# A two-layer graph network on one core: overflow check, record format and the order in which a one-hot stage begins

## The reference

```python
# layer 0: per edge (row = src, col = dst), w = exp(-edge_weight)
h   = relu(layernorm(x))
x   = x + relu(h @ WS.T + bS + segment_sum((h[dst] @ WN.T + bN) * w[:, None], src))
# layer 1: attention over the edges that end in a node
h   = relu(layernorm(x))
q, k, v = h @ Wq + bq, h @ Wk + bk, h @ Wv + bv
logit = sum(q[dst] * k[src]) / sqrt(128)        # softmax over the edges of each dst
x   = x + elu(segment_sum(alpha[:, None] * v[src], dst) + h @ Ws + bs)
```

## Time and profile before

| | |
|---|---|
| median of 3 executions | 880.79 us (880.11 to 882.0) |
| profiled execution | 879.39 us |
| its span, first to last instruction | 877.6 us |
| TensorE busy | 770.2 us (88%) |
| VectorE busy | 725.2 us (83%) |
| ScalarE busy | 530.8 us (60%) |
| PoolE busy | 255.2 us (29%) |
| mean granted TensorE clock | 0.973 |

### The profile page before, as it was taken

How to read it: one execution, slowest core, us unless ns; L and a number is a source line. 1 busy time by engine, 2 the same in 40 slices (tenths; PEclk the granted TensorE clock), 3 DMA queues, 4 the chain that set the end, 5 groups by cost and what they waited for, 6 DMA issues and landing times.

```text
span 877.6 us, 23043 instructions
## 1 busy us (share of the span) xinstructions
PE 770.2 (88%) x8849; PEld 664.7 (76%) x8896; DVE 725.2 (83%) x883; ACT 530.8 (60%) x1034; POOL 255.2 (29%) x200
## 2 busy tenths in 40 slices
PE   0073899999999999999999777899999999999996
PEld 0052777777777777777776556799999999999996
DVE  6657999999999999999995635778878878878872
ACT  5954767676676766767665352455564565555554
POOL 5640000000000000000000320557657657656666
PEclk9996799999999999999999899899999999999999
DMA  9440113132131311313123602204334334324400
GB/s 231 140 131 2 77 78 150 75 131 94 75 149 75 140 84 84 140 75 149 75 93 132 262 38 75 76 2 156 112 122 155 112 121 155 127 106 155 144 18 11
DMA packets 17516, 94.96 MB, mean 108 GB/s; under 512 B 2594, under 2 KB 8844, under 8 KB 10956
## 3 DMA queue, kind: packets, MB, share of 16 engines
q1 hardware_dynamic: 14428, 89.18, 26.6%
q0 software_dynamic: 3056, 5.35, 2.5%
HBM read 50.31 MB, written 44.21 MB: 108 GB/s over the span
## 4 chain that ended last, share of the span: by engine, by line
PE 66%; DVE 16%; issue 10%; ACT 4%; POOL 1%; DMA 1%; DVEq 1%; POOLq 0%; SPq 0%; ACTq 0%
PE bank L1167 16%; PE bank L1177 14%; PE bank L1027 13%; DVE oh_key L872 6%; PE bank L1017 5%; PE bank L1089 5%; PE bank L1087 4%; PE bank L1164 3%; DVE kT L776 3%; PE bank L1131 2%; PE bank L1136 1%; ACT kT L510 1%; ACT qT L502 1%; DVE mx L948 1%; DVE oh_lo L869 1%
## 5 line engine op out<-in xcount | busy, mean ns | idle before, releaser
L456 POOL TENSOR_TENSOR sm<-sm,mbc 128x896 f32<-128x896 f32 (+1 forms) x100 | 186.0, 1892 | 47.2 <-ACT mbc L646 47.2
L1087 PE MATMUL bank<-oh_key,oh_lo 128*128 128x100 bf16 x1600 | 173.5, 210 | 12.7 <-DVE oh_key L872 11.4
L1027 PE MATMUL bank<-wsb,hvb 128*128 128x512 f32 (+1 forms) x350 | 165.2, 577 | 14.4 <-DVE kT L776 13.2
L1167 PE MATMUL bank<-qT,kT 128*128 (+1 forms) x1250 | 170.6, 278 | 3.6 <-DVEq L170 1.2
L1089 PE MATMUL bank<-oh_key,oh_lo 128*128 128x50 bf16 x3200 | 173.7, 188 | 0.0
L1167 PEld LDWEIGHTS bank<-qT,kT 128*128 128x128 f32 x1250 | 167.5, 195 | 5.0
L1087 PEld LDWEIGHTS bank<-oh_key,oh_lo 128*128 128x128 bf16 x1600 | 156.6, 98 | 18.7 <-DVE oh_key L872 11.6
L1089 PEld LDWEIGHTS bank<-oh_key,oh_lo 128*128 128x128 bf16 x3200 | 167.0, 98 | 1.1
L650 ACT ACTIVATE sm<-sm 128x896 f32<-128x896 f32 (+1 forms) x100 | 86.7, 867 | 108.9 <-POOL sm L456 108.9
L552 ACT COPY wsb<-bank 128x512 f32<-128x512 f32 (+1 forms) x175 | 87.9, 552 | 106.2 <-PE bank L1017 106.2
L1177 PE MATMUL bank<-vals,sm 128*128 128x129 f32 x1250 | 147.5, 274 | 0.2 <-ACT sm L650 0.2
(11 more groups left out here) (120 smaller groups left out, 725.4 us busy)
## 6 DMA issues: line engine op xcount, KB each, us to landing
gt<-gst SPq DMA_DIRECT2D x25, 1600.0 KB, 5.6
gl_sb<-gt SPq DMA_DIRECT2D x25, 1600.0 KB, 6.7
records<-rec SPq DMA_DIRECT2D x1, 1612.0 KB, 6.1
out<-res SPq DMA_DIRECT2D x24, 64.0 KB, 1.6
dst_i<-in_dst SPq DMA_DIRECT2D x1, 403.0 KB, 5.8
dstn_i<-in_dst_next SPq DMA_DIRECT2D x1, 403.0 KB, 6.8
src_i<-in_src SPq DMA_DIRECT2D x1, 403.0 KB, 7.3
w_in<-in_edge_weight SPq DMA_DIRECT2D x1, 403.0 KB, 8.0
```

Of the source, the lines that this page charges most:

```text
L456: pool.tensor_tensor(part, part, mbc[:, v % 2:v % 2 + 1, :].to_broadcast([P, n, P]), ALU.subtract).then_inc(sub_done, 1)
L1027: T.matmul(ps(6 + at)[:, 0:n], hvb[:, w, :], wsb[:, at, 0:n], start=True, stop=True).then_inc(l0_mm, 1)
L1087: T.matmul(cells, lo, oh_key[:, u, m, 0:2 * KEYS, i], start=True, stop=False, skip_group_check=True)
L1167: ins = T.matmul(score_bank(g)[:, j * P:(j + 1) * P], kT[:, (a + j) * P:(a + j + 1) * P], qT[:, bass.ds(t * P, P)], start=False, stop=True ...
```

## The change

- **The check.** The host gives a third array, `dst_far`: the destination of the edge 128 further on. VectorE marks edges for which it is not above their own destination with the lowest bit set, and edges whose successor is lower. ScalarE sums both marks, TensorE adds the sums, and the flag is written before any window is fetched. `open_windows` has no `over` any more, and a window is 128 records.
- **The branch.** Each engine reads the flag and branches where it stands; `end_stage(1)` is gone, and a new barrier, `start_slow`, is in the slow branch alone.
- **The records.** Five fp32 words (20 bytes in place of 16): key (destination times 25 plus the high source bits), low bits, three weight parts. The windows are transposed as fetched, by a view of the upper half of each word; VectorE only subtracts the pair's offset from the keys.
- **The layer norm.** ScalarE does the sums and squares of 17 tiles, VectorE the other eight with its batch-norm statistics.
- **The order.** One-hots begin when block 0 is turned. Ahead of tile 0's groups stand the features, window group 0 and four of seven neighbour groups; the other neighbour groups, window groups 1 to 4 and the self features are put between the groups of tiles 0 and 1 on TensorE and ScalarE. ScalarE copies the neighbour features, PoolE adds their bias.
- `gst` and `wst` are two tensors each, in the order gst0, wst0, gst1, wst1.

```diff
-WIN = SLOTS + 1
-REC = 8
-R_LO, R_HI, R_W = 2, 3, 4
+WORDS = 5
+W_KEY, W_LO, W_W = 0, 1, 2
...
-EARLY = 1
+LN_ACT = 17
+LN_DVE = NT - LN_ACT
...
-records = nc.dram_tensor("records", (EP + TAIL, REC), BF16).ap()
+records = nc.dram_tensor("records", (EP + TAIL, WORDS), F32).ap()
...
-    sp.dma_start(dst_i[:], dst.rearrange("(p c) -> p c", p=P)).then_inc(s_dst, 16)
-    sp.dma_start(dstn_i[:], dst_next.rearrange("(p c) -> p c", p=P)).then_inc(s_dst, 16)
     sp.dma_start(src_i[:], src.rearrange("(p c) -> p c", p=P)).then_inc(s_src, 16)
     sp.dma_start(w_in[:], edge_weight.rearrange("(p c) -> p c", p=P)).then_inc(s_w, 16)
+    sp.dma_start(dst_i[:], dst.rearrange("(p c) -> p c", p=P)).then_inc(s_dst, 16)
+    sp.dma_start(dstn_i[:], dst_next.rearrange("(p c) -> p c", p=P)).then_inc(s_far, 16)
+    sp.dma_start(dstf_i[:], dst_far.rearrange("(p c) -> p c", p=P)).then_inc(s_far, 16)
...
+    def neighbour_features():
+        pool.wait_ge(s_wts, 16 * 12)
+        for n, (a, k) in enumerate(TG):
+            pool.wait_ge(s_hnev, n + 1)
+            pool.tensor_tensor(hv[:, a:a + k, :], hv[:, a:a + k, :], brow[:, 0:1, :].to_broadcast([P, k, D]),
+                               ALU.add).then_inc(s_hvb, 1)
+
+    with pool.If(slow):
+        neighbour_features()
+        start_slow(pool)
+    with pool.Else():
+        pool.wait_ge(s_recst, 32)
+        for g, (a, n) in enumerate(WG):
+            pool.wait_ge(s_start, g + 1)
+            for k in range(a, a + n):
+                pool.indirect_dma_start(win[:, k, :], None, records,
+                                        bass.IndirectOffsetOnAxis(start_i[:, k:k + 1], 0)).then_inc(s_win[g], 16)
+        neighbour_features()
...
+    act.wait_ge(s_split, 1)
+    nc.scalar.copy(rec[:, :, W_LO], src_lo[:]).then_inc(s_rec, 1)
+    for k in range(2):
+        act.wait_ge(s_part, 2 * k + 1)
+        nc.scalar.copy(rec[:, :, W_W + k], part_b[:, k, :]).then_inc(s_rec, 1)
...
+    for t in range(LN_ACT):
         nc.scalar.activation(kt3[:, t, :], xs[:, t, :], ACT.Identity, accum_out=nmean[:, t:t + 1]).then_inc(s_sum, 1)
+    for k in range(2):
+        act.wait_ge(s_badt, k + 1)
+        nc.scalar.activation(bad_e[:, k, :], bad_e[:, k, :], ACT.Identity, accum_out=bad[:, k:k + 1]).then_inc(s_bad, 1)
     act.wait_ge(s_ln, 1)
-    for t in range(NT):
+    for t in range(LN_ACT):
         nc.scalar.activation(qt3[:, t, :], xs[:, t, :], ACT.Square, bias=nmean[:, t:t + 1],
                              accum_out=rstd[:, t:t + 1]).then_inc(s_sum, 1)
-    act.wait_ge(s_sum, 2 * NT)
+    act.wait_ge(s_sum, 2 * LN_ACT)
+    act.wait_ge(s_lnd, 2)
     nc.scalar.activation(rstd[:], rstd[:], ACT.Sqrt, bias=eps_col[:, 0:1], scale=1.0 / D).then_inc(s_std, 1)
-
-    act.wait_ge(s_ln, 3)
-    for n, (a, k) in enumerate(TG):
+    act.wait_ge(s_flag, 1)
+    slow = act.value_load(flag[0:1, 0:1], min_val=0, max_val=1)
...
+                if isinstance(t, int) and t == 0 and j == 3:
+                    act_neighbours(4, len(TG))
+                    take_windows(1, 3)
+                if isinstance(t, int) and t == 0 and j == 7:
+                    act_self(0, 4)
+                    take_windows(3, 5)
+                if isinstance(t, int) and t == 1 and j == 1:
+                    act_self(4, NPC)
+                    act.wait_ge(s_hvb, len(TG))
...
+        act_features(0, 3)
+        take_windows(0, 1)
+        act_features(3, len(TG) + 1)
+        act_neighbours(0, 4)
         act_tile(0, 0, 0, False)
-        with act.Fori(0, NT // 2) as i:
+        act_tile(1, 1, 0, True)
+        act_tile(2, 0, 1, True)
...
+    look_up(2)
+    dve.wait_ge(s_part, 2)
+    V.tensor_copy(part_b[:, 1, :], rest[:]).then_inc(s_part, 1)
+    dve.wait_ge(s_part, 3)
+    V.tensor_tensor(rec[:, :, W_W + 2], rest[:], part_b[:, 1, :], ALU.subtract).then_inc(s_recw, 1)
+    dve.wait_ge(s_dst, 16)
+    dve.wait_ge(s_split, 2)
+    V.scalar_tensor_tensor(out=rec[:, :, W_KEY], in0=dst_i[:], scalar=float(NT), in1=src_hi[:], op0=ALU.mult,
+                           op1=ALU.add).then_inc(s_recw, 1)
+    look_up(3)
+    step(V.tensor_scalar(odd_i[:], dst_i[:], 1, None, ALU.bitwise_or))
+    dve.wait_ge(s_far, 32)
+    V.tensor_tensor(bad_e[:, 0, :], dstn_i[:], dst_i[:], ALU.is_lt).then_inc(s_badt, 1)
+    V.tensor_tensor(bad_e[:, 1, :], dstf_i[:], odd_i[:], ALU.is_le).then_inc(s_badt, 1)
+    look_up(4)
+    V.tensor_copy(ident[:], ctab[:, P:2 * P]).then_inc(s_id, 1)
+    V.tensor_copy(ident_b[:], ctab[:, P:2 * P]).then_inc(s_id, 1)
+    V.tensor_scalar(minus_b[:], ctab[:, P:2 * P], -1.0, None, ALU.mult).then_inc(s_id, 1)
+    dve.wait_ge(s_sum, LN_ACT)
+    V.tensor_scalar(nmean[:, 0:LN_ACT], nmean[:, 0:LN_ACT], -1.0 / D, None, ALU.mult).then_inc(s_ln, 1)
+    count_chunks(0)
+    dve.wait_ge(s_badsum, 1)
+    V.tensor_scalar(flag[:], ps(6)[0:1, 0:1], 1.0, None, ALU.min).then_inc(s_flag, 1)
+    dve.wait_ge(s_x, 32)
+    for t in range(LN_DVE):
+        last = V.bn_stats(ln_st[:, t, :], xs[:, LN_ACT + t, :])
+    step(last)
+    for t in range(LN_DVE):
+        last = V.bn_aggr(ln_mv[:, t, :], ln_st[:, t, :])
+    step(last)
+    V.tensor_scalar(nmean[:, LN_ACT:], ln_mv[:, :, 0], -1.0, None, ALU.mult).then_inc(s_lnd, 1)
+    V.tensor_scalar(rstd[:, LN_ACT:], ln_mv[:, :, 1], float(D), None, ALU.mult).then_inc(s_lnd, 1)
+    count_chunks(1)
+    count_chunks(2)
+    dve.wait_ge(s_std, 1)
+    V.reciprocal(mean[:], rstd[:]).then_inc(s_ln, 1)
+    dve.wait_ge(s_ln, 2)
+    dve.wait_ge(s_lnd, 1)
+    V.tensor_tensor(nmean[:], nmean[:], mean[:], ALU.mult).then_inc(s_ln, 1)
+    count_chunks(3)
+    count_chunks(4)
...
-        step(V.tensor_tensor(ahead[:, blocks, :], win32[:, blocks, 0:SLOTS, 0],
-                             nid[:, blocks].unsqueeze(2).to_broadcast([P, n, SLOTS]), ALU.subtract))
-        V.scalar_tensor_tensor(out=over[:, blocks], in0=win32[:, blocks, SLOTS, 0], scalar=-1.0, in1=nid[:, blocks],
-                               op0=ALU.add, op1=ALU.is_le).then_inc(s_over, 1)
-        V.scalar_tensor_tensor(out=xin_field(F_KEY)[:, blocks], in0=ahead[:, blocks, :], scalar=float(NT),
-                               in1=win_field(R_HI)[:, blocks], op0=ALU.mult, op1=ALU.add).then_inc(s_xin, 1)
-        for f, cell in ((F_LO, R_LO), (F_W, R_W), (F_W + 1, R_W + 1), (F_W + 2, R_W + 2)):
-            V.tensor_copy(xin_field(f)[:, blocks], win_field(cell)[:, blocks]).then_inc(s_xin, 1)
-
-    for g in range(EARLY):
-        open_windows(g)
-
-    dve.wait_ge(s_wts, 16 * 12)
-    for n, (a, k) in enumerate(TG):
-        dve.wait_ge(s_hn, n + 1)
-        V.tensor_tensor(hv[:, a:a + k, 0:D], ps(2 + n % 2)[:, 0:k * D].rearrange("p (t f) -> p t f", f=D),
-                        brow[:, 0:1, :].to_broadcast([P, k, D]), ALU.add).then_inc(s_hnev, 1)
-
-    for g in range(EARLY, len(WG)):
-        open_windows(g)
-    dve.wait_ge(s_over, len(WG))
-    step(V.tensor_reduce(bad[:, 1:2], over[:], AX, ALU.add))
-    V.tensor_reduce(badsum[:], bad[:], AX, ALU.add).then_inc(s_bad, 1)
-    dve.wait_ge(s_badsum, 1)
-    V.tensor_scalar(flag[:], ps(6)[0:1, 0:1], 1.0, None, ALU.min).then_inc(s_flag, 1)
+        V.tensor_tensor(xin[:, blocks, :], win32[:, blocks, :, W_KEY],
+                        nid[:, 1, blocks].unsqueeze(2).to_broadcast([P, n, SLOTS]), ALU.subtract).then_inc(s_xin, 1)
...
+        open_windows(0)
         dve.wait_ge(s_tab, 2)
-        dve_tile(0, 0, False)
+        dve.wait_ge(s_xtev, 1)
+        quad(0, 0, 0, [], [])
+        open_windows(1)
+        open_windows(2)
+        quad(0, 0, 1, [], [])
+        open_windows(3)
+        open_windows(4)
         dve_tile(1, 1, False)
+        dve.wait_ge(s_xtev, NB)
+        dve.wait_ge(acc_ev, NPC)
...
+                if isinstance(t, int) and t == 0 and j == 2:
+                    pe_neighbours(4, len(TG))
+                    turn_windows(1, 3)
+                if isinstance(t, int) and t == 0 and j == 6:
+                    pe_self(0, 4)
+                    turn_windows(3, 5)
+                if isinstance(t, int) and t == 1 and j == 0:
+                    pe_self(4, NPC)
+                    pe.wait_ge(acc_ev, NPC)
+                    pe.wait_ge(s_xtev, NB)
...
+        turn_features(0, 3)
+        turn_windows(0, 1)
+        turn_features(3, len(TG))
+        pe_neighbours(0, 4)
+        pe.wait_ge(s_hT, len(TG))
...
+    far = _layout(np.asarray(dst)[SLOTS:], EP - E + SLOTS, 2 * PAD_NODE)
```

319 lines of the change are left out of this document (163 added, 156 removed).

## The result

The changed kernel took **870.11 us** (median of 4, 869.1 to 872.17) against 880.45 (median of 4) for the kernel before: ratio 0.9883, interval [0.986, 0.9906], 10.3 us faster. The forecast was 862.2 us, a gain of 18.6, and a range that ends at 870. The profiled execution took 869.59 us, span 867.8, which is 9.8 less than the span before.

What follows compares the result with a forecast made beforehand. TensorE and VectorE bound the one-hot stage, so only tile 2's start moves: 88.0 against 106.58, 18.6 us gained, 879.39 to 860.8 profiled, 862.2 against the median. Range 857.5 (3 and 1.5 less) to 870 (3, 2 and 3 more).

Steps and rivals of the forecast that it cites:

- Steps 1 and 2: Records and layer norm: feature sums begin at about 20 us, then sums, check, squares and a gap end at 36.1.
- Step 3: Branch on the flag: the barrier goes, register load and jump cost ScalarE 1.6 us, reaching 37.7.
- Step 4: Features and first tile: TensorE's first one-hot group at 58.5 us instead of 88.12, with 1.2 of waiting for window transposes.
- a first one-hot at 43 to 46: Sign at the head of the one-hot stage: the first one-hot comes at 43 to 46 us.
- Step 5: Old work paid back in tiles 0 and 1: 24.6 us on ScalarE plus about 4 of restarts, 28.6 together.
- All later stages shifted by the same amount: Sign after tile 2: 15.6 us a tile, and every later stage moved by the same amount.
- The slow clock in tiles 0 and 1: Rival: TensorE stays slow through the first two tiles, adding 8 us, for 870; chance 0.08.
- PoolE and VectorE in each other's way: Second rival, tiles 0 and 1: PoolE's bias additions block the one-hots, adding seven times 1.0 us, for 869; chance 0.05.
- The steady loop takes a slower step: Rival, one-hot stage: a ring between TensorE and VectorE locks at 16.6 us a tile, adding 23, for 885; chance 0.05.

Runs made afterwards that it cites:

- rep_after: The changed kernel run once more, unedited: 860.55 us.
- before_store: The kernel before the change, with the attention stage's rows stored one step later: 879.59 us against 880.53, ratio 0.9987.
- unheld_again: The changed kernel with rows stored one step later and window gathers not held back, run beside the held version: 859.21 us.
- store_late_again: The changed kernel with the attention stage's rows stored one step later, run once more: 859.92 us.
- after_again: The changed kernel once more, unedited, in several executions beside padded versions on the same chip; its own time is not stated in the text.
- dead_64: The changed kernel with 64 never-executed instructions put into ScalarE's slow branch: all four executions 861.87 to 862.92 us.
- late_gather_store: The changed kernel with window gathers 1 to 4 held until ScalarE's first two window copies, and rows stored one step later: 864.01 us.
- held_again: The changed kernel with window gathers held back and rows stored one step later, run once more: 863.83 us.
- late_gather: The changed kernel with window gathers 1 to 4 held until ScalarE's first two window copies: profiled execution 860.83 us, the other four 867.51 to 868.37.
- late_weights: The changed kernel with the twelve weight and bias transfers issued after the store of the records: 867.80 us (865.76 to 871.59).

## Why the prediction was wrong, point by point

**Steps 1 and 2** held. Squares from 26.77 us (about 27), flag at 27.72 (29), normalisation at 36.14 (36.1). The two accumulations took 0.87 us each (1.0) and the fp32 copies 1.64 to 1.67 (1.61). **Step 3** was 1.6 too long: the normalisation was to follow the jump at 37.7 and starts at 36.14, released by VectorE's nmean 1.09 us after ScalarE was ready. The register load and the jump cost nothing that can be seen beside VectorE's reciprocal.

**Step 4** is the first that failed. Its terms were close, but it had one wait of "about 1.2 of waiting for the window transposes", and this wait is 1.27 us in executions like rep_after and 7.51 in the profiled one. Without it the first one-hot group starts at 54.90 and not 58.5, since ScalarE starts step 4 at 35.26 for 37.7 and TensorE needs 3.9 us behind ScalarE's last feature copy where I gave it 4.9; with it, at 62.25. So the step was 3.6 us too late for one kind of execution and 3.75 too early for the other. The profiled execution was of the second kind, and by their times (869.1 to 872.17) so were the other three, of which there is no trace. The first sign, a first one-hot at 43 to 46, already missed: it came at 50.10 (42.99 in rep_after). That a transpose signals promptly is right in 9 of the 18 profiles. The kernel before pays little for it: before_store has missing updates too, and its copy waits 1.42 us with no releaser named, and starts at 57.65 for 55.49, but its first one-hot group comes at 88.9 for 88.1. There much other work stands between the two; the change put these copies directly ahead of the one-hots.

**Step 5** held: 28.8 us from the first group (62.25) to tile 2 (91.05), forecast 28.6; the same 28.8 in rep_after, 54.90 to 83.72. The gain to tile 2 is 15.53 in the one and 22.86 in the other; the forecast 18.6 lies between them by chance, for in neither did step 4 go as forecast.

**"All later stages shifted by the same amount"** is the other step that failed. It was written for stages that nothing touches. The one-hot stage did shift (15.53 at tile 2, 15.03 at tile 24), but the attention stage took 5.87 us back: 1.87 in its first two steps (13.77 and 13.79 for 12.70 and 12.99), the other 4.00 in the ring of SyncE's load and store. The first two go with the clock. In eight of the 18 profiles the granted clock is 0.75 over both, and they take 13.5 to 13.8 us; in the other ten, the two of the kernel before and that of before_store among them, it is 0.86 or 0.87, and they take 12.4 to 13.0. Windows over the first step, of rep_after and of unheld_again:

```profile
518.00:532.00 14.00, 10.38 (x64) 9.49 (x64) 10.21 (x9) 3.18 (x3) 0.38 (x1) 0.76 0.33 117
```

```profile
520.00:534.00 14.00, 10.26 (x75) 9.51 (x74) 11.46 (x8) 3.41 (x4) 2.23 (x2) 0.88 0.41 132
```

In both it falls to its lower level once in each of the two steps, for 6.8 us in the one and 3.4 in the other. Both kinds occur with one and the same program (store_late_again has 13.7 and 13.8 us, unheld_again 12.4 and 13.0), so these 1.87 us are not the work of the change alone. Why the clock falls longer at one time than at another was not tried.

**The rivals.** The slow clock in tiles 0 and 1 did not come in the profiled execution: from 62.25 on a slot takes 0.10 us, full speed. In after_again and dead_64 it fell for a short part of tile 0, and in two of the three profiles with the gathers held it came behind the second rival. *PoolE and VectorE in each other's way* came and cost nothing in the profiled execution. Line 447 on PoolE:

```profile
L447 POOL TENSOR_TENSOR hv<-hv,brow x7: 1212/2027/5127, 60.1 to 75.1; 128x512 f32<-128x512 f32 x6, 128x128 f32<-128x128 f32 x1
```

The seven additions took 16.30 us where I had 7.0, and the set of one-hots beside them, from 67.51 on in VectorE's timeline above, 9.62 us (77.13 - 67.51) where the next took 5.9 for the same five instructions. But VectorE then waited 8.04 us for TensorE ahead of tile 2. It had room, as the argument against that rival said, though in tile 1 and not where the argument looked for it. In late_gather_store and held_again it had none, and there the rival came in full. The Trainium skill (SBUF — State Buffer, Who interferes with whom) says that a VectorE instruction with two SBUF inputs contends with GpSimd's reads; the trace agrees, with VectorE's set at 1.6 times its length and PoolE's additions at 2.3 us on average for the 1.0 that I had estimated (1.26 where PoolE was not held up). *The steady loop takes a slower step* was refuted with the words "the ring has no memory of its start, if the work of each turn is the same". For the one-hot stage that is so. For the attention stage it is wrong: its ring of loads and stores has one, and I had not looked for rings in stages that the diff doesn't touch. The same page and section of the Trainium skill says of the pair of ports that, against a VectorE instruction in a mode that uses both, whoever issues first has it "for the whole instruction". In which mode the diag runs no run here shows; in effect the trace agrees (1.18 us for 0.29, ended with PoolE's last subtraction). A bf16 input did not avoid it.

**The size.** From the forecast gain of 18.6 to the 9.8 of the profiled execution: 3.1 are lost ahead of tile 2 (15.53 for 18.6; in rep_after it is 22.86, and the first group and with it tile 2 are 7.3 later in the profiled execution), 5.9 in the attention stage, and about 0.15 come back elsewhere. An execution without the late signals has 22.9 at tile 2, loses 4.1 in the attention stage, and takes 860.55. That this is the forecast for a profiled execution, 860.8, is luck: there tile 2 came 4.3 us sooner than forecast, and the attention stage, which was to keep its length, took 4.1 back.

**The range.** Its bounds were added up slightly wrong: 862.2 - 3 - 1.5 is 857.7 and not 857.5, and 862.2 + 3 + 2 + 3 is 870.2 and not 870. The measured 870.11 lies between the two upper figures, which says nothing for the sum, because none of the three terms in it is what the time was spent on.

**Open** is what makes the signals late. It lasts from about 15 us to the end of the window gathers (near 50 us, in before_store near 58), shows in every profile of two sessions and in none of three others, and in both kernels. It is neither ScalarE's program nor the time of the weights' transfers. The updates of that stretch are thinned out in the trace at the same time, so it may be that the signals and their record use one path and that recording takes part in it; no run here is without the recording, so this was not tried.

## What to carry to other kernels

When work moves to the head of the chain, its waits count there in full: price each hand-over on the new chain with the worst that it showed anywhere, not with its usual time. A stage that the change does not touch still need not keep its length; look in it for a ring through a queue in which a load stands behind a store, and for an instruction of VectorE that comes close to the end of one of PoolE's. If there is such a ring, cut it first (here: store one step later, 2.4 to 4.0 us, and every step behind the first two at 13.0 us), then measure the change. And where PoolE works beside one-hots that TensorE will soon want, look at how long a single product takes while they overlap: with the same work on both engines it was 2.1 us in late_gather's profile and 8.8 in late_gather_store's.

## What was not expected of the hardware

- TensorE's update of a semaphore came 3.3 to 6.6 us after the transpose that carries it, against 0.33, for transposes at 42 to 43 us, and the trace lacked several hundred updates of the stretch around it.
- A TENSOR_SCALAR of 128 columns on VectorE, 0.29 us alone, took up to 1.33 us while PoolE's TENSOR_TENSOR ran (late_weights), and up to 0.99 with a bf16 operand.
- An fp32 addition of 128x512 on PoolE took up to 5.13 us beside VectorE's one-hots, which kept their 0.98 us; the median of the seven is 2.03.
- The other way round, a bf16 TENSOR_TENSOR of 128x1600 on VectorE, 0.98 us alone, took 8.79 us while seven such additions ran at 1.26 us (late_gather_store).
- Holding the window gathers back by a few us brought about that meeting, and with it a granted clock of 0.66 over 10 us, 4 to 5 us in all.
